# Tridiagonalising a 512 x 512 matrix: the column norm read out of the matrix product, and the step's masks and sums on VectorE instead of GpSimd

## What is computed

```python
def _layernorm(x, axis=-1, eps=1e-05):
    m = jnp.mean(x, axis=axis, keepdims=True)
    v = jnp.var(x, axis=axis, keepdims=True)
    return (x - m) / jnp.sqrt(v + eps)
...
        h = jax.nn.relu(jnp.einsum('ts,bsh->bth', adj, x @ Wg0 + bg0))
        h = jax.nn.relu(jnp.einsum('ts,bsh->bth', adj, h @ Wg1 + bg1))
...
        deg = jnp.sum(A, axis=0) + jnp.sum(A, axis=1) - jnp.diagonal(A)
        d_inv_sqrt = jnp.where(deg > 0, jax.lax.rsqrt(deg), 0.0)
        L = jnp.diag(deg) - A
        L_norm = d_inv_sqrt[:, None] * L * d_inv_sqrt[None, :]
        _, U = jnp.linalg.eigh(L_norm)
        agg = jnp.einsum('mn,bnd->bmd', U.T, features)
        h = jax.nn.relu(agg @ W1 + b1)
        out = h @ W2 + b2
        return jnp.einsum('nm,bmd->bnd', U, out)
    x = _layernorm(x + _L0_gnn_ref(x, adj, ...), axis=-1)
    x = _layernorm(x + _L1_gnn_ref(x, adj, ...), axis=-1)
```

## Time and profile before

| | us |
|---|---|
| median of 3 runs | 6162.72 (6158.05 to 6484.39) |
| the profiled execution | 6150.05 |
| its span in the profile | 6147.9 |
| DVE busy in the span | 4304.7 |
| PE busy in the span | 3290.3 |
| POOL busy in the span | 790.6 |
| first to last L961 (510 steps) | 894.0 to 3608.0 |

### The profile page before, as it was taken

The page is one execution under the profiler, slowest core; times in us unless marked ns, Lnnn a source line. Parts: engine busy times, 40 slices in busy tenths (PEclk is TensorE's granted clock), DMA queues, the critical chain, the costliest instruction groups (busy, mean ns, idle before and its releaser), DMA issues.

```text
span 6147.9 us, 78861 instructions
## 1 busy us (share of the span) xinstructions
PE 3290.3 (54%) x19000; PEld 2342.0 (38%) x19000; DVE 4304.7 (70%) x27212; ACT 932.4 (15%) x4314; POOL 790.6 (13%) x3424
## 2 busy tenths in 40 slices
PE   7877738888888888777777730000002212230476
PEld 4333226565566666666666630000002212120243
DVE  1222286666677777888888889999968888889534
ACT  2432201111122222222222210000000000000000
POOL 0000001111111111111100014444430000000000
PEclk9988855555555555555555555555555555565578
DMA  2000000000000000000000000000000000000000
GB/s 55 0 0 0 0 0 1 1 1 1 1 1 1 1 1 1 1 1 1 1 1 1 1 1 1 1 1 1 1 1 0 0 0 0 0 0 0 0 0 27
DMA packets 20805, 17.38 MB, mean 3 GB/s; under 512 B 6544, under 2 KB 16784, under 8 KB 20368
## 3 DMA queue, kind: packets, MB, share of 16 engines
q1 hardware_dynamic: 20368, 12.65, 0.8%
HBM read 8.41 MB, written 4.20 MB: 2 GB/s over the span
## 4 chain that ended last, share of the span: by engine, by line
DVE 53%; PE 37%; issue 6%; ACT 2%; SPq 1%; POOL 0%; DMA 0%; DVEq 0%; ACTq 0%; POOLq 0%
PE bank L487 9%; PE bank L436 5%; PE bank L499 5%; PE bank L491 3%; DVE qp L1193 2%; PE bank L470 2%; PE bank L438 2%; DVE ycol L934 2%; DVE dif L1546 2%; PE bank L482 2%; DVE ts L966 1%; DVE qp L1183 1%; DVE tau_row L950 1%; DVE jcol L958 1%; DVE gated L948 1%
## 5 line engine op out<-in xcount | busy, mean ns | idle before, releaser
L487 PE MATMUL bank<-lapw,hid 128*32 128x160 f32 (+3 forms) x10200 | 660.3, 421 | 61.2 <-DVE lapw L907 17.8
L524 PE MATMUL bank<-diag,blk 128*128 128x32 f32 (+1 forms) x96 | 23.3, 416 | 1041.4 <-DVE diag L1310 1030.0
L487 PEld LDWEIGHTS bank<-lapw,hid 128*32 128x32 f32 x10200 | 395.1, 163 | 190.7 <-DVE lapw L969 83.0
L499 PE MATMUL bank<-xp,ones 128*128 128x1 f32 x1020 | 298.9, 362 | 277.9 <-DVE xp L958 277.9
L524 PEld LDWEIGHTS bank<-diag,blk 128*128 128x128 f32 x96 | 21.4, 327 | 1043.5 <-DVE diag L1310 1031.9
L219 POOL TENSOR_TENSOR sq<-hid,ltm 128x4 f32<-128x4 f32 (+3 forms) x510 | 101.0, 198 | 2324.3 <-DVE hid L961 2265.7
L497 PE MATMUL bank<-xp,ones 128*128 128x1 f32 x1020 | 299.0, 362 | 185.4 <-DVE xp L940 185.4
L436 PE MATMUL bank<-hid,onehot 128*128 x504 | 328.2, 769 | 120.0 <-DVE ga L736 67.2
L499 PEld LDWEIGHTS bank<-xp,ones 128*128 128x128 f32 x1020 | 255.3, 311 | 321.6 <-DVE xp L958 321.6
L497 PEld LDWEIGHTS bank<-xp,ones 128*128 128x128 f32 x1020 | 255.3, 311 | 229.1 <-DVE xp L940 229.1
L470 PE MATMUL bank<-xn,ones 128*128 128x2 f32 x1020 | 299.3, 363 | 18.5 <-DVE xn L887 17.6
(11 more groups left out here) (729 smaller groups left out, 8493.1 us busy)
## 6 DMA issues: line engine op xcount, KB each, us to landing
out_x<-xs SPq DMA_DIRECT2D x16, 256.0 KB, 3.3
lapw<-in_adj SPq DMA_DIRECT2D x1, 1024.0 KB, 5.9
bias_rows<-in_L_gnn_bg SPq DMA_DIRECT2D x8, 64.0 KB, 5.6
hid<-lz SPq DMA_DIRECT2D x32, 1.0 KB, 1.7
bias_rows<-in_L_gnn_b SPq DMA_DIRECT2D x4, 64.0 KB, 5.7
wg<-in_L_gnn_Wg SPq DMA_DIRECT2D x2, 64.0 KB, 11.0
wg<-in_L_gnn_W SPq DMA_DIRECT2D x2, 64.0 KB, 3.6
xs<-in_x SPq DMA_DIRECT2D x1, 0.5 KB, 19.7
```

Source lines behind the costliest of these rows:

```text
L487: m = pe.matmul(bank[1][32 * q:32 * q + 32, 0:(T + 1) * 32].rearrange("p (u i) -> p u i", i=32), acols[:, t, k:k + 1].to_broadcast([P, 32] ...
L499: pe.matmul(bank[2][:, 4 * NB:4 * NB + 1], ones[:, 0:P], xp[:, 1:2], start=True, stop=True).then_inc(vp_ps, 1)
```

## The change

The step is written anew. The product now multiplies the matrix, and two extra panel columns at the current place (j), with a: before the product GpSimd puts the unit vector e(k+1) into the first (L223) and a masked to the rows below the diagonal into the second (L225). The product then holds alpha and the squared norm of the masked a beside y. Panel and reflections are kept with the masked a in place of v; the unit vector's share is put in by scalars. `norms` with its PE pass (L470), GpSimd's squares (L219 to L232) and their PE pass (L495) are gone. DVE reads alpha and the norm from the product (`al`, L895), ACT takes the root, GpSimd makes two small coefficients (L228, L229). Masking (`yam`, L918) and picking the element at the diagonal (L909, L917) are on DVE. Two passes on PE remain for sums: L492 (two columns) and L494 (three columns). After the loop some row operations on 510 elements are added to put the tridiagonal matrix and v together. Lines in this paragraph are those of the changed kernel. In the diff leading blanks are cut, and so are declarations, the code after the loop, and the removed lines of the DVE loop (L910 to L970 above).

```diff
@@ buffers and names, in part @@
-        acols, gate_row = mix, vrow
+        acols = vcols
...
@@ -210,26 +211,22 @@
 link(pool.memset(zt[:], 0.0))
 pool.memset(spare[:, 0:1], 0.0).then_inc(vt_clear, 1)
-linked = 0
 for k in range(STEPS):
-    t0 = (k + 1) // P
+    t0, j = (k + 1) // P, k % NB
+    T = NT - t0
+    if k == 0:
+        pool.wait_ge(a_ready, 1)
+    else:
+        pool.wait_ge(y_done, k)
+    if j == 0 and k:
+        pool.wait_ge(panx_ps, k // NB)
+    pool.tensor_copy(pan[:, t0:, :, j, 0], onehot[:, t0:, k + 1].unsqueeze(2).to_broadcast([P, T, 4])).then_inc(am_ready, 1)
     pool.wait_ge(a_ready, k + 1)
-    if k:
-        pool.wait_ge(tail_ps, k)
-    pool.tensor_tensor(sq[:, 0, t0:], acols[:, t0:, k], ltm[:, t0:, k + 1], ALU.mult).then_inc(tail_link, 1)
-    linked += 1
-    pool.wait_ge(tail_link, linked)
-    if t0 == NT - 1:
-        pool.tensor_tensor(xn[:, 2:3], sq[:, 0, t0:], sq[:, 0, t0:], ALU.mult).then_inc(tail_in, 1)
-    else:
-        pool.tensor_tensor(sq[:, 1, t0:], sq[:, 0, t0:], sq[:, 0, t0:], ALU.mult).then_inc(tail_link, 1)
-        linked += 1
-        for t in range(t0 + 1, NT - 1):
-            pool.wait_ge(tail_link, linked)
-            pool.tensor_tensor(sq[:, 1, t:t + 1], sq[:, 1, t:t + 1], sq[:, 1, t - 1:t], ALU.add).then_inc(tail_link, 1)
-            linked += 1
-        pool.wait_ge(tail_link, linked)
-        pool.tensor_tensor(xn[:, 2:3], sq[:, 1, NT - 1:], sq[:, 1, NT - 2:NT - 1], ALU.add).then_inc(tail_in, 1)
+    pool.tensor_tensor(pan[:, t0:, :, j, 1], acols[:, t0:, k].unsqueeze(2).to_broadcast([P, T, 4]),
+                       ltm[:, t0:, k + 1].unsqueeze(2).to_broadcast([P, T, 4]), ALU.mult).then_inc(am_ready, 1)
+    pool.wait_ge(al_ready, k + 1)
+    pool.tensor_scalar(coef[:, 1:2], al[:, 0:1], al[:, 0:1], al[:, 1:2], ALU.mult, ALU.add).then_inc(coef_ready, 1)
+    pool.tensor_scalar(coef[:, 0:1], al[:, 0:1], 0.0, 0.5, ALU.is_ge, ALU.subtract).then_inc(coef_ready, 1)
 pool.memset(spare[:, 1:2], 0.0).then_inc(rot_used, 1)
 pool.memset(spare[:, 2:3], 0.0).then_inc(rot_used, 1)
 for w in range(SWEEPS):
@@ -302,27 +299,27 @@
 for k in range(STEPS):
     t0, j = (k + 1) // P, k % NB
-    T = NT - t0
-    act.wait_ge(norm_ps, k + 1)
-    act.activation(ts[:, 0:1], bank[0][:, 0:1], ACT.Sqrt).then_inc(norm_root, 1)
-    if k:
-        act.wait_ge(w_ready, k)
-        act.activation(swap[:, t0:, (k - 1) % NB, 1], pan[:, t0:, 0, (k - 1) % NB, 0], ACT.Copy).then_inc(w2_ready, 1)
     if j == 0 and k:
         act.wait_ge(panx_ps, k // NB)
         act.activation(panx[:, 0, t0 * P:], bank[1][0:2 * NB, t0 * P:], ACT.Copy)
         act.activation(panx[:, 1, t0 * P:], bank[2][0:2 * NB, t0 * P:], ACT.Copy).then_inc(panx_sb, 1)
         act.wait_ge(updated, k // NB)
+    if k == 0:
+        act.wait_ge(a_ready, 1)
     act.activation(tz[:, t0:, 0], lap[:, t0:, k + 1], ACT.Copy).then_inc(edge_ready, 1)
-    act.wait_ge(x_ready, k + 1)
-    act.activation(swap[:, t0:, j, 0], vcols[:, t0:, k], ACT.Copy)
-    act.activation(pan[:, t0:, :, j, 1], vcols[:, t0:, k].unsqueeze(2).to_broadcast([P, T, 4]), ACT.Copy).then_inc(v2_ready, 1)
+    act.wait_ge(am_ready, 2 * k + 2)
+    act.activation(swap[:, t0:, j, 0], pan[:, t0:, 0, j, 1], ACT.Copy).then_inc(v2_ready, 1)
+    act.wait_ge(al_ready, k + 1)
+    act.activation(root[:], al[:, 0:1], ACT.Sqrt, scale=al[:, 0:1], bias=al[:, 1:2]).then_inc(norm_root, 1)
+    act.wait_ge(g_ready, k + 1)
     act.wait_ge(p_ready, k + 1)
-    act.activation(w0[:, t0:], pcol[:, t0:], ACT.Copy, scale=tau_row[:, k:k + 1]).then_inc(w0_ready, 1)
-    act.wait_ge(a_ready, k + 2)
-    act.activation(vyrow[:, k:k + 1], bank[3][:, 0:1], ACT.Copy).then_inc(vy_saved, 1)
-act.wait_ge(w_ready, STEPS)
-act.activation(swap[:, NT - 1:, (STEPS - 1) % NB, 1], pan[:, NT - 1:, 0, (STEPS - 1) % NB, 0], ACT.Copy).then_inc(w2_ready, 1)
+    act.activation(w0[:, t0:], pcol[:, t0:], ACT.Copy, scale=gt[:, 0:1]).then_inc(w0_ready, 1)
+    act.activation(wts[:, 2:3], gt[:, 1:2], ACT.Copy).then_inc(g_copied, 1)
+    act.activation(gt_row[:, k, :], gt[:, 0:2], ACT.Copy)
+    act.activation(p_row[:, k:k + 1], wts[:, 1:2], ACT.Copy)
+    act.wait_ge(w_ready, k + 1)
+    act.activation(swap[:, t0:, j, 1], pan[:, t0:, 0, j, 0], ACT.Copy).then_inc(w2_ready, 1)
+    act.activation(ends_row[:, k, :], bank[0][:, 0:2], ACT.Copy).then_inc(vy_saved, 1)
 act.activation(tz[:, NT - 1:, 0], lap[:, NT - 1:, N - 1], ACT.Copy).then_inc(edge_ready, 1)
 for w in range(SWEEPS):
@@ -466,13 +463,11 @@
 for k in range(STEPS):
     t0, j = (k + 1) // P, k % NB
     T, c0 = NT - t0, t0 * P
-    pe.wait_ge(norm_in, 2 * (k + 1))
-    pe.matmul(bank[0][:, 0:2], ones[:, 0:P], xn[:, 0:2], start=True, stop=True).then_inc(norm_ps, 1)
     if k:
         pe.wait_ge(w_ready, k)
-        pe.wait_ge(v2_ready, k)
     if j == 0 and k:
         pe.wait_ge(w2_ready, k)
+        pe.wait_ge(v2_ready, k)
         for t in range(t0, NT):
             pe.transpose(bank[1][0:2 * NB, t * P:(t + 1) * P], lapw[:, t, N:N + 2 * NB], ident[:])
             m = pe.transpose(bank[2][0:2 * NB, t * P:(t + 1) * P], swap[:, t, :, :].rearrange("p j s -> p (j s)"), ident[:])
@@ -481,6 +476,8 @@
         for t in range(t0, NT):
             pe.matmul(bank[4 + t][:, c0:], panx[:, 0, t * P:(t + 1) * P], panx[:, 1, c0:], start=True, stop=True).then_inc(update_ps, 1)
         pe.wait_ge(updated, k // NB)
+    pe.wait_ge(a_ready, k + 1)
+    pe.wait_ge(am_ready, 2 * k + 2)
     for t in range(t0, NT):
         strips = lapw[:, t, c0:].rearrange("p (u q i) -> p u q i", q=4, i=32)
         for q in range(4):
@@ -491,15 +488,12 @@
         pe.matmul(bank[2][:, 0:2 * j], unit(k), lapw[:, t0, N:N + 2 * j], start=True, stop=True).then_inc(rowz_ps, 1)
     if k:
         pe.wait_ge(vy_saved, k)
-    pe.wait_ge(tail_in, k + 1)
-    pe.matmul(bank[4][:, 0:1], ones[:, 0:P], xn[:, 2:3], start=True, stop=True).then_inc(tail_ps, 1)
-    pe.wait_ge(x_ready, k + 1)
-    pe.matmul(bank[3][:, 0:1], ones[:, 0:P], xp[:, 0:1], start=True, stop=True).then_inc(vy_ps, 1)
+    pe.wait_ge(x_ready, 2 * k + 2)
+    pe.matmul(bank[3][:, 0:2], ones[:, 0:P], xd[:, 1:3], start=True, stop=True).then_inc(vy_ps, 1)
     pe.wait_ge(x2_ready, k + 1)
-    pe.matmul(bank[2][:, 4 * NB:4 * NB + 1], ones[:, 0:P], xp[:, 1:2], start=True, stop=True).then_inc(vp_ps, 1)
+    pe.matmul(bank[0][:, 0:3], ones[:, 0:P], xd[:], start=True, stop=True).then_inc(vy2_ps, 1)
 j = STEPS % NB
 pe.wait_ge(w_ready, STEPS)
-pe.wait_ge(v2_ready, STEPS)
 pe.matmul(bank[2][:, 0:2 * j], unit(STEPS), lapw[:, NT - 1, N:N + 2 * j], start=True, stop=True).then_inc(rowz_ps, 1)
 pe.wait_ge(diag_in, 1)
 for t in range(NT):
...
@@ -907,66 +891,65 @@
             m = V.tensor_tensor(lap[:, t, c0:], lap[:, t, c0:], bank[4 + t][:, c0:], ALU.add)
         m.then_inc(updated, 1)
...
     dve.wait_ge(y_done, k + 1)
+    V.tensor_scalar(al[:], bank[1][:, here:here + 2], 1e-36, None, ALU.add).then_inc(al_ready, 1)
     a = put(V.tensor_tensor(yz[:, t0:, 0:32], bank[1][:, 0:T * 32].rearrange("p (t i) -> p t i", i=32),
                             pick[:].unsqueeze(1).to_broadcast([P, T, 32]), ALU.mult))
     if j:
         dve.wait_ge(w2_ready, k)
...
         a = put(V.tensor_tensor(yz[:, t0:, 32:32 + 2 * j], panel_cols(j, t0), panel_rows(bank[1][:, T * 32:T * 32 + 32], j, T), ALU.mult))
+    after(a)
+    y = put(V.tensor_reduce(ya[:, t0:, 1], yz[:, t0:, 0:32 + 2 * j], AX.X, ALU.add))
+    dve.wait_ge(edge_ready, k + 1)
+    if j:
         rowz += 1
         dve.wait_ge(rowz_ps, rowz)
         c = put(V.tensor_tensor(tz[:, t0:, 1:1 + 2 * j], panel_cols(j, t0), panel_rows(bank[2], j, T), ALU.mult))
...
+    after(y)
+    V.tensor_tensor(xd[:, 2:3], ya[:, t0, 1:2], ident[:, e:e + 1], ALU.mult).then_inc(x_ready, 1)
+    V.tensor_tensor_reduce(jcol[:, 0, t0:], a_, ya[:, t0:, 1], 1.0, 0.0, ALU.mult, ALU.add, xd[:, 1:2]).then_inc(x_ready, 1)
     if j:
         after(c)
...
+    V.tensor_reduce(ya[:, t0:, 0], tz[:, t0:, 0:1 + 2 * j], AX.X, ALU.add).then_inc(a1_ready, 1)
+    dve.wait_ge(norm_root, k + 1)
+    r = put(V.reciprocal(ts[:, 0:1], root[:]))
+    dve.wait_ge(a1_ready, k + 1)
+    V.tensor_tensor(xd[:, 0:1], ya[:, t0, 0:1], ident[:, e:e + 1], ALU.mult).then_inc(x2_ready, 1)
+    V.tensor_tensor(yam[:, t0:, :], ya[:, t0:, :], ltm[:, t0:, k + 1].unsqueeze(2).to_broadcast([P, T, 2]), ALU.mult).then_inc(a1_masked, 1)
+    dve.wait_ge(coef_ready, 2 * k + 2)
+    after(r)
+    r = put(V.tensor_scalar(ts[:, 1:2], ts[:, 0:1], coef[:, 1:2], root[:], ALU.mult, ALU.add))
+    after(r)
+    p = put(V.tensor_tensor(wts[:, 1:2], ts[:, 1:2], coef[:, 0:1], ALU.mult))
+    after(p)
+    q = put(V.tensor_scalar(wts[:, 0:1], al[:, 0:1], wts[:, 1:2], coef[:, 1:2], ALU.mult, ALU.add))
+    dve.wait_ge(a1_masked, k + 1)
     if k:
         dve.wait_ge(w0_ready, k)
...
+    V.scalar_tensor_tensor(pcol[:, t0:], yam[:, t0:, 0], wts[:, 1:2], yam[:, t0:, 1], ALU.mult, ALU.add).then_inc(p_ready, 1)
+    after(q)
```

(19 more changed lines are left out.)

110 lines of the change are left out of this document (37 added, 73 removed).

## The result

The changed kernel takes 6313.69 us (median of 4 runs, 6308.44 to 6318.82); the kernel before took 6161.50 on the same chip. The ratio is 1.0249, with 1.0229 to 1.0269 as its interval: 2.5% slower. One of the four executions of the kernel before (6484.39 us) fell in a slower state and is left out of the ratio. The time lies inside the predicted range, 74 us above the predicted 6240. It is slower by more than 2%, an outcome that the forecast had given a chance of 0.29, against 0.66 for a difference within 2%. The profiled execution took 6315.33 us, with a span of 6313.6.

A forecast was written before the change was run, and what follows sets the result against it. No engine is full; step length decides: the product plus DVE's row in series, 5.13 us against 4.97. 6150.05 + 82 - 12 + 5 = 6225 for the profiled execution, 6238 at the median, stated as 6240; range 6160 to 6350.

The forecast's parts named there:

- The bound and the series: Each step: the product plus DVE's whole row in series, nothing of DVE beside the product; 5.13 us against 4.97.
- The size by tiles: Step length by column tiles: about 0.3 us more with four and three, 0.2 with two, 0.1 less with one.
- L936's waits: The column without its last term, waiting for the gate with two semaphores: bounds 0 and 0.07 us more, 0.035 taken.
- PE's start and GpSimd's copy: End of step: PE starts 0.05 us after w; GpSimd's copy of a into the panel hidden, by 0.05.
- The sign that the prediction named for a late copy: Before the product: DVE stands ready and PE's wait in front of L484 is for `am_ready`.
- L907: Where DVE asks for the panel row: with one tile the row comes some 0.05 us late, 0.01 in the mean.
- ACT's copy: Behind the gate, needed by the three-element dot at 0.71 us: there at 0.63, hidden by some 0.1.
- The blocks: Block steps: transposes no longer wait behind the next norm's root; 12 us less over 31 blocks, between 0 and 20.
- 1: Step's end: GpSimd's copy and DVE's last write hold each other up; 0.21 us a step, 107 us, 6347; chance 0.17.
- Rival 2: Waits on DVE's own semaphores cost 0.10 us each, not 0.03: 89 us, 6329, with half 6285; chance 0.12.
- Rivals 3 and 4: 3: DVE's row packs tighter, 6171, chance 0.17; 4: product cheaper as the granted clock rises, 5910, chance 0.03.
- The parts outside the loop: After the loop: about ten small and long row operations more, 5 us.

The follow-up runs named there:

- a_swap_all: Changed kernel with the waits at L936 and L907 turned to put the pending one first, and PE's wait for w put last: 6292.89 us, ratio 1.0217.

## Why the prediction was right, and where it was short

- *The bound and the series*: right. DVE is idle beside the whole product and starts 0.06 after it; the pivot beside the product instead of behind it is worth 271 us in the changed kernel and costs 338 us in the one before. The change removes a pass and the wait for the panel row and puts about a microsecond of DVE's chain behind the product.
- *The size by tiles*: 6.4, 5.4, 4.6 and 4.1 were forecast, 6.51, 5.52, 4.74 and 4.27 came, each 0.11 to 0.17 short. It was to be 0.1 less than before with one tile, and was 0.03 more.
- *L936's waits*: the mis-sized term. I knew the two bounds, 0 and 0.07 more, and took the middle because GpSimd might have been the cause in the earlier trace rows. It was 0.09 more. Turning the two waits round gave 30 us.
- *PE's start and GpSimd's copy*: wrong, and small. PE's start was taken as 0.05 behind w or behind the copy, whichever came last, from the earlier trace rows, and the copy as hidden by 0.05: 0.23 + 0.08 + 0.20 + 0.05 = 0.56 against 0.61. But PE starts 0.145 after the copy and not 0.05, so the copy's row is 0.66 and ends last, by 0.05. That is the 0.05 a step by which PE is late, 25 us. The sign that the prediction named for a late copy (the profile puts PE's wait down to `am_ready`) did not show it, since w ended last by the profile.
- *L907*: forecast 0.05 late with one tile. With the pending wait in front it is 0.03 late by the row; the order of its two waits adds 0.07. The rest of that piece, some 0.04 in the mean, lies between L895 and L909 in all sizes and was not taken apart by a run.
- *ACT's copy*: hidden, but not by the 0.1 of the prediction. When it has to wait for the copy, L944 starts 0.14 after its end; in the change it starts 0.17 after. So 0.03 was left, and with L936 in time it is gone.
- *The blocks*: wrong. A block's gap exceeds a step's by 10.99, 7.33, 4.47 and 2.36 us, where it was 10.94, 7.20, 4.25 and 2.19. With 7 blocks of the first size and 8 of each other that is 5 us more, not 12 less.
- *The rivals*: 1 falls with the six GpSimd operations. The Trainium skill, "SBUF — State Buffer", on the shared port pair, has the loser blocked for the whole instruction; operations of 1 to 16 elements do not show it here. One place may be touched by it: in the step shown, L910, which starts 0.01 after GpSimd's L223, took 0.19 where it takes 0.15 elsewhere. With one tile it takes over 0.17 in 48 of 127 steps of the change, and in none of the version with ACT's early copy, where L223 starts 0.04 after it; the price is up to 0.04 us, not the 0.18 that was left of L223. Rival 2 gave the right size, 6285 to 6329, by the wrong cause: a wait on DVE's own semaphore costs 0.03, unless a satisfied one stands in front of it. Rivals 3 and 4 did not occur.

From the table of pieces, 0.13 us times 510 is 66 us, and the blocks add 17. The parts outside the loop took 9 us more where 5 were allowed. That makes 87, and the profiled executions lie 165 us apart where the forecast had 75: 90 are missing there. Only 74 are missing between the medians, because the 15 us allowed for the step from the profiled execution to the median and for PE's waits did not come: 16 us of luck. The orders of waits and of ACT's copy, with one wait of PE dropped, were worth 53 us; PE's 25 us, the price of the copy, are seen but not removed.

## What to carry to other kernels

Before a chain is moved behind a long operation to save a pass, add up what stood beside that operation; here a saved pass of 0.60 us and a saved wait were paid with the whole pivot in series. Where an instruction has two waits, put the one that will be pending first, and count a start whose pending wait stands behind a satisfied one as 0.07 to 0.09 us later, as measured here. Where two events come close together, the profile's releaser is the one that ended last, not always the one that was waited for: look for the distance that stays the same from step to step. And look for two-pointer instructions on the bound: splitting one, so that a product is formed beside something else, was worth 46 us.

## What the runs showed of the hardware

- A satisfied wait in front of a pending one: DVE starts 0.10 to 0.12 after the event (L886, L936, L907); with the pending one first, 0.03. On PE 0.15 against 0.05 (w's wait last in `a_swap_all`, first in the kernel before). Three such waits in 510 steps cost 68 us.
- PE's product starts 0.145 us after the end of GpSimd's copy in every version in which the copy's wait stands last, with each number of tiles.
- GpSimd operations of 4 elements with two SBUF inputs run beside DVE's with next to no change of DVE's: six a step, 5 us of 6314.
- An operation with two pointers takes 0.27 on DVE for one element, and a product of two columns 0.16; on GpSimd it was 0.34 against 0.20 (L228, L225). ACT's root with a pointer scale and bias takes 0.39, where the root without them took 0.17 in the kernel before (L307) and ACT's copies in the same step take 0.19.
